# Attention inside a four-layer network: positional value products spread over the next block, relative terms in a new order

## The reference, cut to what matters

```python
qk = einsum('nhcp,nhci->nhpi', q, k)
qr = einsum('nhcp,cpi->nhpi', q, q_pos) * gate_qr
kr = einsum('nhcp,cpi->nhpi', k, k_pos) * gate_kr
att = softmax((bn(concat([qk, qr, kr]))).reshape(-1, 3, heads, H, H).sum(1), axis=-1)
att_v  = einsum('nhpi,nhci->nhcp', att, v * gate_v)
att_vp = einsum('nhpi,cpi->nhcp', att, v_pos * gate_v_pos)
```

## Time and profile before

| what | value |
|---|---|
| median of three executions | 17333.0 us |
| the profiled execution's own time | 17346.83 us |
| its span | 17345.0 us |
| mean granted TensorE clock, as a share of 2.4 GHz | 0.837 |
| TensorE matmul busy, share of the span | 73% |
| VectorE / ScalarE / GpSimd busy | 55% / 32% / 50% |
| the attention stage's blocks | from about 2251 to 5242 us |

### The profile page before, as it was taken

The page is one execution under the profiler, slowest core; times in us unless marked ns, Lnnn a source line. Parts: engine busy times, 40 slices in busy tenths (PEclk is TensorE's granted clock), DMA queues, the critical chain, the costliest instruction groups (busy, mean ns, idle before and its releaser), DMA issues. The chain is left out here.

```text
span 17345.0 us, 233377 instructions
## 1 busy us (share of the span) xinstructions
PE 12681.1 (73%) x80914; PEld 7160.2 (41%) x80914; DVE 9531.3 (55%) x14944; ACT 5526.5 (32%) x7813; POOL 8648.0 (50%) x8027
## 2 busy tenths in 40 slices
PE   5554378888880057767767776776688999999998
PEld 2553145555550045555555555554223333333333
DVE  4556878888883423333333333333126777777777
ACT  1112444444440000000000000000106777777776
POOL 0112411111111057777777777776006777777777
PEclk9999976666665578888888888887899999999999
DMA  4113333333325954454454444333422021110201
GB/s 98 36 28 67 86 60 53 56 54 53 56 50 161 203 149 126 125 135 126 125 139 121 125 125 128 111 110 103 85 60 39 20 49 22 32 37 20 49 21 31
DMA packets 1324675, 1419.97 MB, mean 82 GB/s; under 512 B 514353, under 2 KB 1065537, under 8 KB 1308545
## 3 DMA queue, kind: packets, MB, share of 16 engines
q1 hardware_dynamic: 1031872, 755.61, 21.0%
q0 software_dynamic: 221184, 604.27, 12.1%
q10 hardware_dynamic: 70976, 50.83, 0.9%
HBM read 1049.46 MB, written 276.84 MB: 76 GB/s over the span
## 5 line engine op out<-in xcount | busy, mean ns | idle before, releaser
L1447 POOL DMA_INDIRECT dc_g<-corners,dc_idx x4608 | 4387.1, 952 | 1366.7 <-issue 1326.4
L1529 PE MATMUL dc_ps<-ident,dc_s 128*128 128x128 f32 x20480 | 2861.0, 311 | 1373.2 <-DVE dc_s L1621 1373.2
L2074 POOL TENSOR_TENSOR df_sq<-df_sq 128x512 f32<-128x512 f32 x1920 | 2519.2, 1324 | 1945.3 <-ACT df_sq L2022 1900.1
L1529 PEld LDWEIGHTS dc_ps<-ident,dc_s 128*128 128x128 f32 x20480 | 2813.9, 226 | 1410.8 <-issue 758.9
L2169 DVE SCALAR_TENSOR_TENSOR df_pr<-df_pk,vecs,df_h 128x512 f32<-128x512 f32 x2880 | 2092.8, 742 | 613.1 <-PE df_pk L1963 343.7
L2022 ACT ACTIVATE df_sq<-df_pk,vecs 128x512 f32<-128x512 f32 x2880 | 1936.0, 685 | 979.2 <-DVE df_pr L2169 956.3
L1621 DVE TENSOR_TENSOR dc_s<-dc_g,dc_pt 128x2304 f32<-128x2304 f32 x512 | 1296.5, 2552 | 1652.7 <-DMA dc_g<-corners,dc_idx 1158.6
L756 POOL TENSOR_TENSOR at_md<-at_mt,at_own 64x512 bf16<-64x512 f32 x256 | 327.5, 1279 | 2663.0 <-DVE at_mt L975 2663.0
L1483 ACT ACTIVATE dc_st<-dc_ps 128x512 f32<-128x512 f32 x640 | 327.0, 607 | 4146.6 <-PE dc_ps L1529 4146.6
L1960 PE MATMUL df_pk<-df_t,df_wp 64*128 64x512 f32 x3840 | 1351.0, 641 | 213.9 <-ACT df_sq L2022 156.7
L949 DVE SCALAR_TENSOR_TENSOR at_x<-at_pq,hconst,at_x 128x256 f32<-128x256 f32 x2048 | 1114.7, 617 | 371.9 <-PE at_pq L793 213.9
(11 more groups left out here) (273 smaller groups left out, 16781.8 us busy)
## 6 DMA issues: line engine op xcount, KB each, us to landing
df_h<-df_h SPq DMA_DIRECT2D x160, 512.0 KB, 7.1
dc_g<-corners,dc_idx POOLq DMA_INDIRECT x4608
corners<-dc_xt SPq DMA_DIRECT2D x90, 512.0 KB, 4.8
at_a<-y SPq DMA_DIRECT2D x192, 192.0 KB
dc_xp<-x SPq DMA_DIRECT2D x32, 1024.0 KB, 20.0
cv_xp<-x SPq DMA_DIRECT2D x8, 4096.0 KB, 49.8
y<-sp_p SPq DMA_DIRECT2D x128, 192.0 KB, 2.8
y<-sp_p SPq DMA_DIRECT2D x64, 384.0 KB, 4.3
```

Source lines behind the costliest of these rows:

```text
L1447: nc.gpsimd.indirect_dma_start(gt[:, r, k, :, :].rearrange("p a c -> p (a c)"), None, image, bass.IndirectOffsetOnAxis(ap=idx[:, s, r, k:k ...
L1529: t = nc.tensor.matmul(ps[:, j, 128 * r:128 * r + 128], sm[:, r % 2, a, 2 * j:2 * j + 2, :].rearrange("p k c -> p (k c)"), env.ident[:, :] ...
L2074: nc.gpsimd.tensor_tensor(a, a, sq[:, (KK * n + other) % RING, :], ALU.add).then_inc(nadded, 1)
```

## The change

The positional part f of block k-1 now stands in quarter f of block k, in two halves of 16 matmuls. In quarters 1 to 3 the first half stands between the two pairs of value products and the second behind the next score products; in quarter 0 both stand behind the turned maxima. Value products always use bank 0 of `pvv`, positional products bank 1. Relative term number r now makes rows 8 * PLACES[r], so that terms 0 to 3 fill the rows that part 0 frees, and so on, and ScalarE waits for one part at every fourth term. Terms 0 and 1 move behind the positional part of quarter 0, term 12 moves from the middle of quarter 3 to its part 2. ScalarE copies one positional part a quarter. On the SP queue `turn(k)` now stores block k-1 and loads v for block k+1.

```diff
+    PLACES = [4 * (r % 4) + r // 4 for r in range(16)]
@@ SP queue
-            def turn(k, s, more=True):
-                if more:
-                    sp.wait_ge(rel_done, 16 * k + 16)
-                    load_relative(k + 2, s)
-                    sp.wait_ge(qk_done, 16 * k + 16)
-                    load(k + 2, s)
-                store(k, s)
-                if more:
-                    load_v(k + 2, s)
+            def turn(k, s, first=False):
+                sp.wait_ge(rel_done, 16 * k + 16)
+                load_relative(k + 2, s)
+                sp.wait_ge(qk_done, 16 * k + 16)
+                load(k + 2, s)
+                if not first:
+                    store(k - 1, 1 - s)
+                    load_v(k + 1, 1 - s)
@@ TensorE
-            def times_vpos(k, s, f, bank, free):
-                if f == 0:
-                    pe.wait_ge(exped, 8 * k + 8)
-                free()
-                for i in range(8):
+            def times_vpos(k, s, f, half):
+                if half == 0:
+                    if f == 0:
+                        pe.wait_ge(exped, 8 * k + 8)
+                    if not (isinstance(k, int) and 4 * k + f < 1):
+                        pe.wait_ge(vp_out, 4 * k + f)
+                for i in range(4 * half, 4 * half + 4):
                     for j in range(4):
...
-                last.then_inc(vp_done, 1)
+                if half == 1:
+                    last.then_inc(vp_done, 1)
-                    p = 8 * r + 2 * i
+                    p = 8 * PLACES[r] + 2 * i
-            RELS = {0: ((), (), (0, 1), ()), 1: ((), (), (2, 3), (4, 5)), 2: ((6,), (7,), (8,), (9, 10)), 3: ((11,), (12,), (13,), (14, 15))}
+            RELS = {0: ((), (), (), (0, 1)), 1: ((), (), (2, 3), (4, 5)), 2: ((6,), (7,), (8,), (9, 10)), 3: ((11,), (), (12, 13), (14, 15))}
...
                     times_v_next((0, 1))
+                    if q:
+                        positional(0)
                     relatives(1)
                     spread_next(2)
                     times_v_next((2, 3))
...
+                    if q:
+                        positional(1)
                     relatives(2)
-                    positional_next((0, 1))
                     transposed_maxima(k, s, q)
+                    if q == 0:
+                        positional(0)
+                        positional(1)
                     relatives(3)
-                    positional_next((2, 3))
@@ ScalarE
-            RELS = {0: ((), ()), 1: ((0, 1), (2, 3, 4, 5)), 2: ((6, 7), (8, 9, 10)), 3: ((11, 12), (13, 14, 15))}
+            RELS = {0: ((), ()), 1: ((0, 1), (2, 3, 4, 5)), 2: ((6, 7), (8, 9, 10)), 3: ((11,), (12, 13, 14, 15))}
                                 if r == 0 and not first:
-                                    act.wait_ge(vp_done, 4 * k)
                                     act.wait_ge(av_done, 4 * k)
+                                if r % 4 == 0 and not first:
+                                    act.wait_ge(vp_done, 4 * k - 3 + r // 4)
...
-                    if q == 0 and not first:
-                        for f in range(4):
-                            vp_to_sbuf(k - 1, 1 - s, f, 1 - f % 2)
+                    if not first:
+                        vp_to_sbuf(k - 1, 1 - s, q)
```

More of the change, by code:

```diff
@@ L732, in _ @@
                 load_v(k, k)
[L734 to L744 removed]
+            def turn(k, s, first=False):
[6 more added lines that the diff above has]
+                    load_v(k + 1, 1 - s)
+            turn(0, 0, True)
+            turn(1, 1)
+            with sp.Fori(1, NBLK // 2 - 1) as v:
                 for s in range(2):
                     turn(2 * v + s, s)
[L747 to L748 removed]
+            store(NBLK - 3, 1)
+            load_v(NBLK - 1, 1)
+            store(NBLK - 2, 0)
+            store(NBLK - 1, 1)
             for s in range(2):
@@ L818, in times_v @@
                     pe.wait_ge(v_arrived[s], 32 * (k // 2 + 1) if isinstance(k, int) else (k - s) * 16 + 32)
-                    free()
+                    if not (isinstance(u, int) and u < 1):
+                        pe.wait_ge(av_out, u)
                 if t % 2 == 0:
@@ L824, in times_v @@
                     at = ((nh % NSEQ) * HEADS + nh // NSEQ) * 9
-                    last = nc.tensor.matmul(pvv[32 * j:32 * j + 9, q % 2, 128 * t:128 * t + 128], vt[:, s, at:at + 9],
+                    last = nc.tensor.matmul(pvv[32 * j:32 * j + 9, 0, 128 * t:128 * t + 128], vt[:, s, at:at + 9],
                                             X[:, s, nh // 2, :, nh % 2], start=True, stop=True, tile_position=(0, 32 * j))
@@ L828, in times_v @@
                     last.then_inc(av_done, 1)
-            def times_vpos(k, s, f, bank, free):
-                if f == 0:
-                    pe.wait_ge(exped, 8 * k + 8)
-                free()
-                for i in range(8):
+            def times_vpos(k, s, f, half):
[5 more added lines that the diff above has]
+                for i in range(4 * half, 4 * half + 4):
                     for j in range(4):
                         p = 32 * j + 8 * f + i
-                        last = nc.tensor.matmul(pvv[32 * j:32 * j + 8, bank, 64 * i:64 * i + 64], pv[:, :, 127 - p],
+                        last = nc.tensor.matmul(pvv[32 * j:32 * j + 8, 1, 64 * i:64 * i + 64], pv[:, :, 127 - p],
                                                 X[:, s, :, p, :], start=True, stop=True, tile_position=(0, 32 * j))
-                last.then_inc(vp_done, 1)
+                if half == 1:
+                    last.then_inc(vp_done, 1)
             def relative(k, s, r):
@@ L890, in relatives, with positional @@
                                 relative(k + 1, 1 - s, r)
-                    def positional_next(fs):
-                        if q == 0 and not first:
-                            for f in fs:
-                                positional(k - 1, 1 - s, f, 1 - f % 2, False)
+                    def positional(half):
+                        if not first:
+                            times_vpos(k - 1, 1 - s, q, half)
                     qk(k, s, q, (2, 3))
@@ L928, in end @@
                     spread(k, 1, 3, t)
-                    times_v(k, 1, 2, t, lambda: pe.wait_ge(av_out, 4 * k + 1))
+                    times_v(k, 1, 2, t)
                 for t in range(4):
-                    times_v(k, 1, 3, t, lambda: pe.wait_ge(av_out, 4 * k + 2))
+                    times_v(k, 1, 3, t)
                 for f in range(4):
-                    positional(k, 1, f, f % 2, True)
+                    for half in range(2):
+                        times_vpos(k, 1, f, half)
             stream(pe, work, start, end)
@@ L1016, in av_to_sbuf @@
                     act.wait_ge(stored[s], stores(k, s))
-                nc.scalar.activation(o1[:, s, 4 * q:4 * q + 4, :], pvv[:, q % 2, :].rearrange("p (a b) -> p a b", a=4),
+                nc.scalar.activation(o1[:, s, 4 * q:4 * q + 4, :], pvv[:, 0, :].rearrange("p (a b) -> p a b", a=4),
                                      ACT.Copy).then_inc(av_out, 1)
@@ L1021, in stores, with vp_to_sbuf @@
                 return 16 * STORES * (k // 2) if isinstance(k, int) else (k - s) * (8 * STORES)
-            def vp_to_sbuf(k, s, f, bank):
+            def vp_to_sbuf(k, s, f):
                 act.wait_ge(vp_done, 4 * k + f + 1)
@@ L1026, in vp_to_sbuf @@
                     act.wait_ge(stored[s], stores(k, s))
-                nc.scalar.activation(o2[:, s, :, 8 * f:8 * f + 8], pvv[:, bank, :].rearrange("p (a n) -> p n a", a=8),
+                nc.scalar.activation(o2[:, s, :, 8 * f:8 * f + 8], pvv[:, 1, :].rearrange("p (a n) -> p n a", a=8),
                                      ACT.Copy).then_inc(vp_out, 1)
-            RELS = {0: ((), ()), 1: ((0, 1), (2, 3, 4, 5)), 2: ((6, 7), (8, 9, 10)), 3: ((11, 12), (13, 14, 15))}
+            RELS = {0: ((), ()), 1: ((0, 1), (2, 3, 4, 5)), 2: ((6, 7), (8, 9, 10)), 3: ((11,), (12, 13, 14, 15))}
             def work(k, s, first, final):
```

26 lines of the change are left out of this document (5 added, 21 removed).

## The result

The changed kernel takes 17289.15 us (13 executions, 17279.74 to 17304.87), the kernel before 17346.49 us beside it (13 executions, 17320.24 to 17361.81). The ratio is 0.9968, with a 95% interval of 0.9959 to 0.9976: 57 us less, where 129 were forecast. The direction was right and the time lies in the range, but the gain is less than half of what the sum said.

The account below looks back on a forecast made before the run. TensorE and VectorE, handing work to each other in attention, bound the kernel, the longer setting each quarter. Blocks of 46.2 us fall to 44.15, the mean of 47.6 and 40.7; 2.05 x 63 = 129 us off gives 17205, range 17050 to 17350.

Parts of the forecast that it names:

- Relative terms in the new order, term 12 moved, ScalarE's waits: nothing: Attention stage: reordered relative terms and ScalarE's added positional copies cost nothing, ScalarE being busy 5.3 to 5.9 of 10 us.
- The 0.5 us a block allowed in the range: Allowance if ScalarE's last relative copies come later and VectorE's 2.51 us wait for them grows.
- The clock: Attention stage: high clock for half the time, block midway between 47.6 us (low) and 40.7 (high), 44.15.
- the forecast's check on the kernel before: Today's block: 47.6 us less 22% of the 6.9 difference between clocks gives 46.1, against 46.2 measured.
- Rival A: Attention stage: clock never comes up without a long positional passage; 46.7 to 48.5 us a block, 17365 to 17480; chance 0.13.
- C: Attention stage: high clock throughout, TensorE hardly ever waiting; 40.7 us a block, 16990 us; chance 0.07.
- The slowed VectorE: Half parts slow subtractions and maxima by the additions' factor 3.1; up to 0.6 us a quarter in three quarters, low clock.
- Rival D: VectorE's subtractions and maxima are not slowed by the parts; 42.05 us a block, 17070 us; chance 0.08.
- TensorE's steps: Attention quarters: a positional part costs 1.9 us at low clock, 1.7 at high; quarter 0 takes 10.9 or 10.0.
- TensorE's wait for the last maximum: Quarters 2 and 3: the 0.57 us wait is used up first, near zero at the low clock.
- the SP queue: Stores and v loads start some 30 us later; six microseconds of slack before v's first reader, so nothing.
- Rival B: Attention stage: high share stays near 22%, VectorE's slowing repays filled gaps; 46.1 us a block, about 17330; chance 0.12.

Follow-up runs that it names:

- the static tile: Changed kernel with positional products reading a static tile of ones, not the maps: 45.36 us a block at step 1024, 43.31 at 1040, 42.86 in a row.
- the late order: Padded changed kernel with relative terms 14 and 15 ahead of quarter 3's turned maxima, positional copy 3 behind the relative copies: 17171.98 us.

## Why the prediction was wrong in its size

**The step that failed** is "Relative terms in the new order, term 12 moved, ScalarE's waits: nothing". Its reason was that ScalarE is busy 5.3 to 5.9 of 10 us in a quarter and that behind the positional copy "only relative copies of the freed rows are queued". Both are true and the conclusion is not: those relative copies free TensorE's two banks, TensorE runs its list in order, and score products stand behind its relative terms. So the copy sits on a path ScalarE, TensorE, VectorE that has no spare time just behind the exponentials, whatever the engine's mean load. The exponentials of that place are slowed too, 1301 ns on average in place of 1052, 1.9 us when a half part lies over them, but that is not what holds TensorE up: with the copy moved they still take 1307 and TensorE's wait for ScalarE is 8 us, and with padding they take 1056 and the wait is 113. The 0.5 us a block allowed in the range was too small; the runs measure (17289 - 17208) / 63 = 1.3. With this one copy moved the block is 44.19 us and the kernel 17208 us, where 44.15 and 17205 were forecast: the other steps hold in their sum. That it comes out to 3 us is luck in part, since terms among them were wrong in both directions (below). That this is the change's own loss and not a gain open to anyone is shown by the kernel before: from 17331 to 17196 with ScalarE's exponentials parted in both and the positional copy moved where there is one, the change is worth 135 us (forecast 129), and 248 with padding in both (17222 to 16974).

**The clock.** Half of the time at the high level, mean 0.75: as forecast (0.504 of the stage). The half was chosen between the bounds and not worked out, so that it fits this closely is luck. Nor was the forecast's check on the kernel before a check: it put 22% at the high clock into 47.6 and 40.7, which are the sums for the changed kernel, and met the old 46.2 by chance. The clock rises 159 times in the stage in place of 60, and the high level has 0.67 and 0.71 of the time of quarters 1 and 3, 0.50 of quarter 2 and 0.20 of quarter 0, which has no part ahead of its turned maxima. Rival A, no rise without a long passage of products, is refuted, as is C. The Trainium skill's rule weighed there ("TensorE: Matmul & The Clock Gate", its part on the clock gate) is that activity releases the throttle. The trace agrees with it as little as before: the second quarter 2 above is busy 10.17 of 10.68 us at 0.68, quarter 1 9.29 of 11.46 at 0.89.

**The slowed VectorE.** Right in kind: subtractions and maxima are slowed as the additions are, by 2.2 and 2.0 where the forecast took 3.1 from a single block; over the whole stage before, the additions that lay wholly beside a part had a median of 1698 ns, and after 1564. Rival D is refuted twice: by the tails above, and by the static tile, with which the step alone decides. The Trainium skill, "SBUF — State Buffer", in its section on the two sides, has a rule behind D, that on the engine side only the port pair shared by GpSimd and VectorE causes contention; the same rows contradict it (subtractions 681 to 1486 ns). What the forecast had not seen is that ScalarE's exponentials are slowed as well, and that the products themselves are. Its price for all this was 2.1 us a block (44.15 less D's 42.05). Padding gives the changed kernel 118 us, 1.9 a block, as it stands. But with ScalarE's list mended it gives 222 us (17196 to 16974), 3.5 a block, and the kernel before 109 (17331 to 17222). So the step of the reads does cost the change more than it costs the kernel before, 113 us more (from the intervals of the four ratios an estimated 55 us to either side); with the copy still in the way the difference was 118 against 107 and did not show.

**TensorE's steps.** Quarter 0 was forecast at 10.9 and 10.0 us and is 11.09, and 10.6 with the copy moved. A half part takes 1.11 us from its start to the next instruction's at the low clock and 1.06 at the high one, where 0.95 and 0.85 were taken. At the low clock, where TensorE sets the pace, that is 0.16 x 8 = 1.3 us a block, for half of the time 0.6; other terms must have been put too high by as much. One is quarter 3, 10.3 forecast and 10.0 with the copy moved; the rest can't be told from the runs. TensorE's wait for the last maximum was to vanish at the low clock; it doubled over the whole. VectorE's slowed work just ahead of it is at most half of the reason: with padding, which takes the slowing away, the wait is still 223.3 us, and 208.8 with ScalarE's order too. The rest of the rise is not explained.

**What was costed at nothing and is nothing.** No value product waits for v in the trace after, so the SP queue had slack enough. VectorE's wait for the last relative terms is 2.6 us a block (166.8 us in 63 blocks), where it was 2.5 (157.9). The measured 17289 lies just outside the band of the forecast itself (17280 to 17130), whose condition, a high clock for a third to two thirds of the stage, was met. Rival B, no change, was nearer in its middle (17330) but not in its reason: the high share did not stay near 22%.

**Still open.** Why padding and ScalarE's list together give more than their sum (315 against 211 us) is only argued: each leaves the other as the next limit. How padding's gain divides between the faster products and the other engines is open as well.

One loss stands in both kernels alike. The waits put 75 us of TensorE's idle time ahead of score products down to nothing that the profile shows, in 19 places (30 us in 6 before). All of them are one place, the first score products behind the jump back to the head of TensorE's loop, in every second block. There, in the changed kernel, TensorE starts a median of 1.04 us after VectorE's additions have released it (0.57 in the kernel before), and 0.05 us in the other kind of block, whose work follows without a jump; it is idle 3.6 and 1.6 us. The view counts such a wait as unexplained only when the release lies more than 1 us back, so the count of places says little. In all, the idle time at this place is 116 us after, 106 before and 108 with the copy moved: hardly any of the 81 us. It is most of what the longer kind of block has more (2.4 us after, 2.0 before). Why the jump costs this, and whether a longer loop body would save it, wasn't tried.

## What to carry to other kernels

Price each instruction that is added to an engine's list by what stands behind it in that list and who waits for that, at the place where it is added; the engine's mean load says nothing about it. When a repair gives less than it should, look whether another limit hides it: padding gave the changed kernel 118 us with the copy in the way and 222 without. And before moving small matmuls about, look at the step of their reads: 16 bytes of padding were worth twice what the change was as first written, and with the change and ScalarE's order they made the kernel 2.1% faster than before (16974.22 us, from 17344.9), the best version found.

## What the runs showed of the hardware that was not expected

- TensorE's reads of its moving operand, 8 bytes every 1024 bytes, slow operations of VectorE, ScalarE and GpSimd that read SBUF meanwhile. With a step of 1040 bytes, the only other one tried, they do not (subtractions at most 694 ns). Medians of operations that lie more than half beside such products against those that lie beside none, worked out from the trace of the changed kernel: additions 1202 (wholly beside them 1564) against 475 ns, subtractions 1486 against 681, maxima 1385 against 699, ScalarE's exponentials 1948 against 1047, GpSimd's placing 2118 against 1039. The last was there before too (2067), where the forecast had looked at VectorE alone. ScalarE's copies from PSUM to rows of the maps, which write SBUF and do not read it, were not slowed (605 against 597).
- The products slow themselves too. A half part takes 1.06 us at the high clock with the step of 1024 and 0.60 with a step of 1040 or none, and at the low clock 1.11 against 1.01: only without the step of 1024 do they profit much from the clock. (These are halves with a relative term right behind them, from start to start.) The groups' rows say it for all of them, in the changed kernel and, with padding and ScalarE's order, in the best version:

```profile
L845 PE MATMUL at_pvv<-at_x,at_pv 128*8 128x64 f32 x16384 | 575.8, 301 | 2.1 <-ACT at_o L1026 2.1
```

```profile
L845 PE MATMUL at_pvv<-at_x,at_pv 128*8 128x64 f32 x16384 | 431.8, 266 | 2.1 <-ACT at_o L1026 2.1
```

- The versions with padding are at the high clock less of the time: 0.50 of the stage after, 0.42 with padding, 0.27 with padding and the late order. Whether part of what padding gives is given back by this, no run shows.
- The program's mean clock differs from one execution to the next, and the time does not show it: two executions of the changed kernel, at 0.808 and 0.860, took 17291.47 and 17290.83 us. In the profiled executions the difference lies in slices 2 to 5, ahead of attention, which read 5 in the changed kernel's at a mean of 0.808, and 9 in that of the version with the copy moved, at 0.861; four of 40 slices at half the clock are an estimated 0.05 of the mean.
- Behind the jump back to its loop's head TensorE starts late, a median of 1.04 us after its release in place of 0.05, worked out from the trace of the changed kernel.
